# A four-layer graph attention kernel: the last layer's scores kept transposed, small steps of the normalisations moved from GpSimd to VectorE, and another order

## The reference

```
h = jnp.maximum(_layernorm(x, axis=-1), 0.0)
x = x + L0(h, adj)      # one head, scores from two vectors, softmax over neighbours, product with h
h = ...; x = x + L1(...)  # L1a: 4 heads of 256, elu; L1b: 1 head of 512
h = ...; x = x + L2(...)  # one head, attention weights on h itself
h = ...; x = x + L3(...)  # 8 heads of 64
```

```
xp = jnp.einsum('bnd,do->bno', x, W_proj)
xh = xp.reshape(B, N, H, k).transpose(0, 2, 1, 3)
a_src = jnp.einsum('bhnk,hk->bhn', xh, W_att[:, :k])
a_dst = jnp.einsum('bhnk,hk->bhn', xh, W_att[:, k:])
scores = a_src[:, :, :, None] + a_dst[:, :, None, :] + b_att[None, :, None, None]
scores = jax.nn.leaky_relu(scores, negative_slope=NEG_SLOPE)
scores = jnp.where(mask, scores, NEG_INF)
att = jax.nn.softmax(scores, axis=-1)
out = jax.nn.relu(jnp.einsum('bhij,bhjk->bhik', att, xh))
```

## Time and profile before

| | us |
|---|---|
| median of three runs | 3213.99 |
| lowest, highest | 3212.21, 3219.64 |
| the profiled execution | 3215.87 |
| its span, first to last instruction | 3213.9 |
| its mean granted clock of TensorE | 0.976 |

### The profile page before, as it was taken

How to read it: one execution, slowest core, us unless ns; L and a number is a source line. 1 busy time by engine, 2 the same in 40 slices (tenths; PEclk the granted TensorE clock), 3 DMA queues, 4 the chain that set the end, 5 groups by cost and what they waited for, 6 DMA issues and landing times.

```text
span 3213.9 us, 77726 instructions
## 1 busy us (share of the span) xinstructions
PE 3052.3 (95%) x21776; PEld 2809.7 (87%) x21776; DVE 2436.3 (76%) x5995; ACT 2413.6 (75%) x6561; POOL 2116.7 (66%) x3236
## 2 busy tenths in 40 slices
PE   1689999999999999999999999999999999999984
PEld 0579999999999999999999999999999999999974
DVE  6477877878787787878778787887878788787752
ACT  2467778878787787877878787887878788787753
POOL 4346666766666676766767666666766677676643
PEclk6899999999999999999999999999999999999986
DMA  4112222222222222222222222222212222222211
GB/s 135 32 46 62 78 63 74 66 64 76 63 78 63 69 71 62 78 63 78 63 69 71 62 78 63 77 64 67 74 62 78 63 75 65 69 72 62 66 39 44
DMA packets 170069, 217.14 MB, mean 68 GB/s; under 512 B 34864, under 2 KB 100528, under 8 KB 169648
## 3 DMA queue, kind: packets, MB, share of 16 engines
q1 hardware_dynamic: 169648, 212.18, 22.2%
HBM read 177.55 MB, written 34.54 MB: 66 GB/s over the span
## 4 chain that ended last, share of the span: by engine, by line
PE 91%; issue 4%; DVE 1%; POOL 1%; ACT 1%; DMA 0%; POOLq 0%; DVEq 0%; ACTq 0%
PE bank_c L365 23%; PE bank_b L365 22%; PE bank_e L365 11%; PE bank_e L691 8%; PE bank_b L513 7%; PE bank_a L409 3%; PE bank_e L655 3%; PE bank_c L591 3%; PE bank_a L435 3%; PE bank_b L507 2%; PE bank_b L358 2%; PE bank_e L358 2%; PE bank_a L396 0%; PE bank_a L422 0%; PE bank_c L579 0%
## 5 line engine op out<-in xcount | busy, mean ns | idle before, releaser
L365 PE MATMUL bank_b<-w_hi,hT_hi 128*128 128x344 f32 x1536 | 470.1, 360 | 7.2 <-DVE hT_lo L1215 6.7
L365 PE MATMUL bank_c<-w_hi,g_hi 128*128 128x258 f32 x2048 | 413.2, 283 | 2.4 <-DVE x L1171 2.4
L365 PE MATMUL bank_c<-w_lo,g_hi 128*128 128x258 f32 x2048 | 413.2, 283 | 0.0
L365 PE MATMUL bank_b<-w_lo,hT_hi 128*128 128x344 f32 x1536 | 410.2, 321 | 0.0
L1474 POOL TENSOR_TENSOR eE<-eE,nmE 128x512 f32<-128x512 f32 x256 | 266.2, 1040 | 178.0 <-DVE nmE L1289 177.0
L1467 POOL TENSOR_TENSOR eE<-t_all_L,mask 128x512 f32<-128x512 f32 x256 | 349.0, 1384 | 32.3 <-DMA t_all_L<-t_dram_L 31.5
L1455 POOL TENSOR_TENSOR g_lo<-g,g_hi 128x512 fp32r<-128x512 f32 x128 | 193.9, 1515 | 262.0 <-ACT g_hi L901 262.0
L365 PE MATMUL bank_c<-w_hi,g_lo 128*128 128x258 f32 x2048 | 363.8, 289 | 0.7
L940 ACT ACTIVATE eE<-eE,st 128x128 f32<-128x128 f32 x1024 | 326.1, 391 | 40.5 <-POOL eE L1467 40.4
L365 PE MATMUL bank_b<-w_hi,hT_lo 128*128 128x344 f32 x1536 | 347.2, 321 | 0.0
L365 PEld LDWEIGHTS bank_b<-w_hi,hT_hi 128*128 128x128 f32 x1536 | 277.7, 189 | 75.0 <-issue 67.1
(11 more groups left out here) (136 smaller groups left out, 8785.5 us busy)
## 6 DMA issues: line engine op xcount, KB each, us to landing
t_all_L<-t_dram_L SPq DMA_DIRECT2D x128, 512.0 KB, 3.9
x_in<-in_x SPq DMA_DIRECT2D x128, 256.0 KB, 2.5
t_all_L1a<-t_dram_L1a SPq DMA_DIRECT2D x128, 256.0 KB, 4.3
out<-out_sb SPq DMA_DIRECT2D x128, 256.0 KB, 4.2
t_all_L<-t_dram_L SPq DMA_DIRECT2D x256, 64.0 KB, 2.9
adj_in<-in_adj SPq DMA_DIRECT2D x128, 64.0 KB, 2.6
t_dram_L1a<-t_rows_L1a SPq DMA_DIRECT2D x512, 0.5 KB
t_all_L1b<-t_dram_L1b SPq DMA_DIRECT2D x128, 64.0 KB, 2.8
```

The costliest lines, as they stand in the source:

```text
L365: last = mm(bank[:, 0:width], a[:, c * P:(c + 1) * P], w[:, c, b * width:(b + 1) * width], start=(first and c == chunks[0] and n == 0), st ...
```

## The change

It has three parts.

*The last layer.* The scores are built with targets down the partitions. The plain mask is transposed on TensorE (`turn_mask_L3`, one bf16 product per graph) and copied by ScalarE (`copy_mask_L3`) to `mask_flat_turned`. The target part becomes the bias column (`tc3`), the source part must now run along the row. The row maximum is needed before the scores exist in the new form: VectorE takes, per source, the maximum over masked targets from the broadcast target rows (`most_L3`, now eight products with a sum's kind of instruction, here add and max), adds the source part and applies the slope (`most_leaky_L3`), which is the maximum of the leaky scores because the slope is monotone. Source part and maximum, 16 columns, are turned into rows (`rows_shift_L3`), stored by four DMAs (`send_shift_L3`) and read back broadcast as `shift_all`, 128 partitions of 16 rows of 128, which is 1 MB (`spread_shift_L3`). GpSimd adds the mask to the source rows and, after the leaky slope, subtracts the maximum rows, both from `shift_all`. The exponentials then are in the form that the product needs: the eight transposes on TensorE and the two copies on ScalarE are gone. The values `xa` get two slots.

*The normalisations.* VectorE adds epsilon in place (`variance`) and makes the bias (`bias`); GpSimd only takes the power (`power`).

*The order.* All five lists are in another order, with smaller distances between the stages of a graph; SKEW is 11. The result is written into `out_sb` directly.

```diff
-SKEW = 12
+SKEW = 11
...
+            def send_shift_L3(g):
+                if g.live:
+                    sp.wait_ge(sem("L3_shift_rows"), g.made())
+                    sp.wait_ge(sem("L3_shift_spread"), 16 * g.made(2))
+                    for b in range(P // Q):
+                        sp.dma_start(shift_dram[g.slot(2), :, b * Q:(b + 1) * Q],
+                                     shift_rows[b * Q:b * Q + 2 * H3, :]).then_inc(sem("L3_shift_sent"), 16)
+
+            def spread_shift_L3(g):
+                if g.live:
+                    sp.wait_ge(sem("L3_shift_sent"), 16 * (P // Q) * g.made())
...
+                    src = shift_dram[g.slot(2):g.slot(2) + 1, :, :]
+                    sp.dma_start(shift_all[:], src.to_broadcast([P, 2 * H3, P])).then_inc(sem("L3_shift_spread"), 16)
...
-            def turn_exp_half_L3(g, i):
-                for k in range(HB):
-                    last = nc.tensor.transpose(bank_e[:, i, k * P:(k + 1) * P], pE[:, i * HB + k, :], ident[:])
-                last.then_inc(sem(f"L3_turned{i}"), 1)
...
+            def turn_mask_L3(t, g):
...
+                    mm(bank_a[:, 0:P], mask[:, g.slot(MR), :], identb[:], start=True, stop=True)\
+                        .then_inc(sem("flat_turned"), 1)
...
+            def copy_mask_L3(g):
+                if g.live:
+                    act.wait_ge(sem("flat_turned"), g.made())
...
+                    activation(mask_flat_turned[:, g.slot(PR), :], bank_a[:, 0:P], ACT.Copy).then_inc(sem("flat_copied"), 1)
...
-            def pT_L3(i, g):
...
+            def variance(layer, g):
+                if g.live:
+                    dve.wait_ge(sem(f"mv_made{layer}"), 2 * g.made() - 1)
+                    ts(mv[layer][:, 1:2], mv[layer][:, 1:2], EPS, None, ALU.add).then_inc(sem(f"mv_made{layer}"), 1)
+
+            def bias(layer, g):
+                if g.live:
+                    dve.wait_ge(sem(f"rs_made{layer}"), 2 * g.made() - 1)
+                    ts(rs[layer][:, 2:3], mv[layer][:, 0:1], rs[layer][:, 1:2], -1.0, ALU.mult, ALU.mult)\
+                        .then_inc(sem(f"rs_made{layer}"), 1)
...
+            def targets_L3(g):
...
+                    nc.vector.tensor_copy(tc3[:], bank_e[:, 1, D // 2:B3]).then_inc(sem("tc3_made"), 1)
...
             def most_L3(i, g):
                 if g.live:
-                    dve.wait_ge(sem(f"L3_leaky{i}"), g.made())
-                    dve.wait_ge(sem(f"L3_shifted{i}"), g.made(1))
-                    half = slice(i * HB, (i + 1) * HB)
-                    nc.vector.tensor_reduce(nmE[:, half], eE[:, half, :], AX_X, ALU.max, negate=True)\
-                        .then_inc(sem(f"L3_max{i}"), 1)
+                    dve.wait_ge(sem("L3_spread"), 16 * g.made())
+                    dve.wait_ge(sem("mask_made"), g.made())
+                    dve.wait_ge(sem("L3_most_leaky"), g.made(1))
+                    for k in range(i * HB, (i + 1) * HB):
+                        last = nc.vector.tensor_tensor_reduce(t_all["L3"][:, k, :], t_all["L3"][:, k, :],
+                                                              mask[:, g.slot(MR), :], 1.0, -3.0e38, ALU.add, ALU.max,
+                                                              most3[:, k:k + 1])
+                    last.then_inc(sem(f"L3_most{i}"), 1)
...
+            def most_leaky_L3(g):
...
+                    tt(most3[:], most3[:], shift_cols[:, 0:H3], ALU.add).then_inc(sem("L3_most_sum"), 1)
+                    dve.wait_ge(sem("L3_most_sum"), g.made())
+                    stt(shift_cols[:, H3:2 * H3], most3[:], SLOPE, most3[:], ALU.mult, ALU.max)\
+                        .then_inc(sem("L3_most_leaky"), 1)
...
+            def power(layer, g):
+                if g.live:
+                    pool.wait_ge(sem(f"mv_made{layer}"), 2 * g.made())
+                    pool.wait_ge(sem(f"rs_made{layer}"), 2 * g.made(1))
                     pool.wait_ge(sem(f"h_made{layer}"), g.made(1))
...
+                    tt(rs[layer][:, 1:2], mv[layer][:, 1:2], nhalf[:], ALU.pow).then_inc(sem(f"rs_made{layer}"), 1)
...
-                    tt(eE[:, half, :], t_all["L3"][:, half, :], m, ALU.add).then_inc(sem(f"L3_masked{i}"), 1)
...
+                    tt(eT[:, half, :], shift_all[:, half, :], m, ALU.add).then_inc(sem(f"L3_masked{i}"), 1)
...
-                    tt(eE[:, half, :], eE[:, half, :], nm, ALU.add).then_inc(sem(f"L3_shifted{i}"), 1)
...
+                    tt(eT[:, half, :], eT[:, half, :], shift_all[:, H3 + i * HB:H3 + (i + 1) * HB, :], ALU.subtract)\
+                        .then_inc(sem(f"L3_shifted{i}"), 1)
```

536 lines of the change are left out of this document (274 added, 262 removed).

## The result

The changed kernel takes 3348.3 us (median of 4 runs, 3345.7 to 3354.0), the kernel before beside it 3214.0 us (4 runs). The ratio is 1.042, with a 95% interval of 1.040 to 1.044: the change costs 134 us. The forecast was 3118 us and its range ended at 3200.

A forecast was written before the change was run, and what follows sets the result against it. TensorE was taken to stay the bound. From 3215.9 us profiled, 119 passes x 0.69 = 82 us and 15 us of fill came off, less 1.9 for the median: 3117, with small waits 3118 us; range 3098 to 3200.

The forecast's parts named there:

- the queue of DMAs: SyncE's added stores and 1 MB broadcast delay masked_L0 and masked_L1a 1 us; costed at nothing, at most 1 us a pass.
- Rival 2: VectorE locked by GpSimd at one reduction and columns_L2, 1.0 us each: pass 24.1 us, about 3275 us; chance 0.12.
- TensorE's part: Last layer: eight transposes go (0.88 us), one mask transpose comes (0.19): net 0.69 us off, pass 22.77 us.
- VectorE's part: Reductions, tiny instructions, a transpose and own waits raise VectorE from 18.8 to 21.6 us in a pass of 22.8.
- GpSimd's part: Normalisations keep only the power, freeing about 3.0 us; layer 3's shifts cost 0.5 more: about 14.9 us a pass.
- The scores for the reductions: Target-score broadcast for VectorE's eight reductions lands at 21.8 us, VectorE arrives at 22.1: fits, barely.
- Fill and drain: Pipeline ends: one pass fewer (SKEW 11 for 12) saves 7.2 us at worst, 22.4 at best; 15 taken.
- its own sign: Fill step is wrong if the mask of graph 9, made at 260.74 us before, comes later than 255 us.
- The check named for the DMAs: DMA step is wrong if GpSimd idles for t_all_L1a or t_all_L0, or VectorE for t_all_L, over 0.3 us a pass.

The follow-up runs named there:

- run 1: Changed kernel with layer 0's 64 KB broadcast (spread_L0) issued ahead of the last layer's 1 MB one on SyncE: 3101.7 us, measured again 3115.2 us.
- run 6: Changed kernel with most_leaky_L3 moved ahead of recip_L1a in VectorE's order: 3365.2 us, ratio 1.045 to the kernel before.
- run 3: Changed kernel with the 1 MB broadcast cut to the 512 KB of source rows, the maxima never sent: 3171.9 us, ratio 0.985 to the kernel before.
- run 7: Changed kernel with the 1 MB broadcast issued by ScalarE, behind elu_first, instead of SyncE: 3309.9 us, ratio 1.029 to the kernel before.
- Run 8: On top of run 1, the 1 MB broadcast cut in two, the 512 KB of maxima sent behind layer 1a's broadcast: 3184.6 us, ratio 0.990.
- run 2: Changed kernel with columns_L2 ahead of most_L0 on VectorE and norm_2 ahead of leaky_L0 on ScalarE, DMAs unchanged: 3184.3 us, ratio 0.989.
- run 4: Changed kernel with the edits of run 1 and run 2 both made: 3181.0 us, ratio 0.989 to the kernel before.

## Why the prediction was wrong, point by point

- **The step that failed: the queue of DMAs.** It read: "a delay of 1 us for `masked_L0` and `masked_L1a` that the order has room for. I cost it at nothing; if the room is gone it is up to 1 us a pass". The size of the transfer was right (1 MB, 6 to 8 us forecast, 7.0 measured). The delay was not 1 us: layer 0's broadcast lands 6.75 us after its issue where it took 2.8 in the kernel before, and is used after 6.9 us behind the 1 MB and 4.9 ahead of it (medians). And there was no room: `most_L0` idled 1.3 us, ScalarE 1.7 us with `exp_L1b`, for which TensorE waits, behind it in its queue. The prediction says nothing of what ScalarE and VectorE have queued behind `masked_L0`. Its cost was put at nothing, or at most 1 us a pass; the one line of run 1 takes 24.74 - 22.72 = 2.02 us a pass away, twice the most that it allowed for. It takes one of the two locks away too, and a late broadcast also delays the next one (run 6). Runs 1, 3 and 7 show it.
- **The rival that came true in part.** Rival 2 named the place, "one more at `columns_L2`, behind `g_lo_last` and `masked_L3_first`", at 1.0 us. It is there, and larger: the two products take 1.65 and 1.54 us in the mean of 1000 to 2000 us where they take 0.73 and 0.69 in the kernel before, 1.8 us a pass, of which 0.9 stay in run 1. Rival 2's pass of 24.1 us is nearer to the 24.74 than any other case, but that is in part luck: it has no late broadcast in it. And it needed no locked reduction. The reductions L1329 were 0.21 us apart, one in eight at 0.44 us, so this fear was misplaced. Nor do the locks come from the late scores: run 3 has the scores in time and both products locked in 41 of 43 passes. What frees one of them in run 1 is that GpSimd then waits for layer 1a's target scores (54.4 us in 1000, for 3.5 in the kernel after). Against rival 2 stood that GpSimd has less to do; what decides is when it does it.
- **TensorE's part** was right, and if anything too small. In run 1, where TensorE is nearly always busy (495.66 of 500), the mean pass is 22.72 us, for 22.77 forecast, waits included. The rows' price of the transposes (0.88 us for eight) held, and not 2.2 us.
- **VectorE's part** was right in size: 457.09 / 500 x 22.72 = 20.8 us busy in run 1, locks included, for 21.6 - 1.4 of own waits = 20.2. The eight reductions take 0.21 us by starts for 0.22 forecast. `most_leaky_L3` takes 0.94 us and not 0.08, by the lock, and run 6 shows that this cost nothing.
- **GpSimd's part** came out at 299.69 / 500 x 24.74 = 14.8 us, and 311.21 / 500 x 22.72 = 14.1 in run 1, for 14.9. But the prediction's own terms, 16.3 - 3.0 + 0.5, give 13.8. The 3.0 us hold idle time between the three chained steps, which isn't in the busy time: busy, the two steps that went took 0.22 and 0.27 us, four times a pass 1.9 us. With that the terms give 14.9. It changed nothing in the forecast, as GpSimd was not the bound.
- **The scores for the reductions**, which I feared to be barely in time, were: VectorE idled 0.7 us in 1000 for `t_all_L` in run 1.
- **Fill and drain** came to -20.0 us (+2.2 and -22.2), for -15, and -24.6 in run 1 (0.0 and 160.0 - 184.6). The size was fair, but by luck: the step failed by its own sign, since the mask of graph 9 comes later than 255 us. The pass that is saved lies ahead of that mask (`make_mask` is now a stage of `t.graph(2)`, where it was `t.graph(3)`), and it saved nothing. The first mask does come 8.3 us earlier (64.42 for 72.67), but the short pass of 7.2 us behind it is now 21.2 us long (the second mask is at 85.60), as the prediction had foreseen. With no short pass left, no more than 7.2 us could be saved there, and not the 22.4 of its best case. The gain lies behind the last mask, where both kernels run nine more passes, and the prediction had no term for it. What makes these shorter was not tested.
- **The check named for the DMAs** pointed at the cause: "GpSimd idles for `t_all_L1a` or `t_all_L0` by more than 0.3 us a pass". It idled 2.1 us a pass ahead of `masked_L0`. But it still does so by 1.6 us in run 1, which takes the time that was forecast: idle time of GpSimd says that the scores are late for GpSimd, and not who stands behind it. The profile names no DMA there, only "issue", so the sign must be read from the distance between SyncE's issue and GpSimd's start.

With that one step mended the total would have stood: run 1 differs from the kernel after by one line of SyncE's order and takes 3101.7 and 3115.2 us in its two measurements, for 3118. Its 118 passes take 88 us less than before, for 82 forecast over 119; the ends take 25 less, for 15.

What stays open: why run 1 took 13 us more in its second measurement (mean pass 22.81 for 22.72), with the kernel before 4 us lower; and whether the last 0.2 us a pass of TensorE's waits (7.1 us in 1000 for `eB`) can be had with the locks avoided too. Run 8 tried one way to it and failed.

## What to carry to other kernels

A large DMA on a shared set of DMA engines is priced by what is asked for behind it: expect each small transfer that is asked for right behind it to land about when the large one does (here 6.75 us after issue, where the 1 MB takes 7.0 and the small one took 2.8 in the kernel before), and ask which engines' in-order queues stand behind the consumer. Issue the small, urgent transfers first; moving the large one to another engine's queue gave 38 of the 247 us here. When a new kernel is slower though no engine is full, look for a chain that closes on itself from one pass to the next, and test a candidate by taking its delay away, because a lock or a long instruction that looks bad may cost nothing (run 6), and a delay that costs much in one order may cost next to nothing in another (runs 2 and 4). Test the two changes together as well as each alone.

## What the runs showed of the hardware that was not expected

- A broadcast of 64 KB issued 0.2 us (run 7) or 0.5 us (kernel after) behind one of 1 MB is used 6.7 and 6.9 us after its issue, from another queue as from the same; issued 0.45 us ahead of it, 4.5 us. Behind 512 KB (run 3) it is 4.8 us, with 0.84 us of GpSimd's waiting. Medians of the landings: 6.75 us behind 1 MB, 6.5 from another queue, 4.8 right ahead of it, 4.4 behind 512 KB, 2.8 in the kernel before. So the place right ahead of a large transfer isn't free either; layer 1b's broadcast, which stands there in the kernel after, lands after 4.7 us, and after 2.9 in run 1, where it is one place further ahead.
- A VectorE product of two SBUF tensors, 128x512, takes 0.68 us, and 1.63 to 1.65 us beside a GpSimd instruction over 128x512. One of 128x8 takes 0.17 us and 0.94. The Trainium skill (SBUF — State Buffer, Who interferes with whom) states the lock; the runs agree and show both sides: GpSimd's instructions grow too (L1529 takes 1.58 us in the mean of the kernel after and 1.29 in run 1, L1506 1.55 and 1.19). In the pass of run 1 that is shown, a wait of 1.51 us of GpSimd gave VectorE 0.95 us back.
